# Attention in float32 on one core: q and k turned by VectorE's blocks and SBUF-to-SBUF transfers instead of TensorE, with plain float32 scores

## What is computed

```python
q = q * cos + _rotate_half(q) * sin
k = k * cos + _rotate_half(k) * sin
scores = einsum('bhqd,bhkd->bhqk', q, k) / sqrt(D)
scores = where(mask == 0, -1e9, scores)
attn = softmax(scores, axis=-1)
x = einsum('bhqk,bhkd->bhqd', attn, v) ... @ Wo
```

## Time and profile before

| | |
|---|---|
| median of 3 runs | 2615.45 us (2614.41 to 2617.41) |
| span of the profiled execution | 2614.6 us |
| TensorE busy | 2382.5 us, 91% |
| VectorE busy | 1786.3 us, 68% |
| GpSimd busy | 1512.2 us, 58% |
| ScalarE busy | 1278.9 us, 49% |
| mean granted TensorE clock | 0.967 |

### The profile page before, as it was taken

How to read it: one execution, slowest core, us unless ns; L and a number is a source line. 1 busy time by engine, 2 the same in 40 slices (tenths; PEclk the granted TensorE clock), 3 DMA queues, 4 the chain that set the end, 5 groups by cost and what they waited for, 6 DMA issues and landing times.

```text
span 2614.6 us, 41410 instructions
## 1 busy us (share of the span) xinstructions
PE 2382.5 (91%) x13005; PEld 2016.6 (77%) x13005; DVE 1786.3 (68%) x3406; ACT 1278.9 (49%) x3698; POOL 1512.2 (58%) x1567
## 2 busy tenths in 40 slices
PE   5899999998889999999887887899689999999977
PEld 4788888886778888888766776776578888888753
DVE  4677777777877777777666676563477777777752
ACT  2555555554246666666534455233245666665421
POOL 5666666665246666666535667423456666666543
PEclk9999999999999999999999999899889999999979
DMA  3234444443224233223310000259513233322344
GB/s 110 80 118 155 141 160 159 151 162 109 71 84 142 97 98 102 93 93 98 109 49 17 1 1 27 81 193 365 175 61 108 91 98 101 101 94 77 116 169 151
DMA packets 191532, 288.12 MB, mean 110 GB/s; under 512 B 15985, under 2 KB 110833, under 8 KB 188378
## 3 DMA queue, kind: packets, MB, share of 16 engines
q1 hardware_dynamic: 175584, 236.34, 27.1%
q0 software_dynamic: 10224, 42.03, 4.6%
q10 hardware_dynamic: 5514, 7.11, 0.9%
HBM read 218.80 MB, written 100.37 MB: 122 GB/s over the span
## 4 chain that ended last, share of the span: by engine, by line
PE 73%; DVE 8%; DMA 6%; POOL 5%; issue 4%; ACT 3%; SPq 0%; POOLq 0%; ACTq 0%; DVEq 0%
PE B_qkv L806 32%; PE B_out L806 19%; PE B_more L883 4%; PE B_s L863 4%; PE B_qT L852 3%; DMA slots_y<-S 3%; PE B_more L806 2%; PE B_s L864 1%; PE B_more L957 1%; DMA out_x<-rows_last 1%; PE B_s L806 1%; DVE xn L1523 1%; DVE X L1650 1%; PE B_qT L806 1%; PE B_more L855 1%
## 5 line engine op out<-in xcount | busy, mean ns | idle before, releaser
L1333 ACT ACTIVATE W<-S,nmx 128x128 f32<-128x128 f32 x768 | 298.1, 395 | 49.9 <-DVE nmx L1625 48.8
L2183 POOL TENSOR_TENSOR S<-S,mask 128x512 f32<-128x512 f32 x184 | 256.6, 1394 | 46.9 <-ACT S L1162 46.9
L1226 ACT ACTIVATE sq<-B_qkv 128x640 f32<-128x640 f32 x127 | 89.7, 706 | 380.1 <-PE B_qkv L806 380.1
L2228 POOL TENSOR_TENSOR pT_l<-W,pT_h 128x512 fp32r<-128x512 f32 x184 | 241.8, 1314 | 32.9 <-ACT pT_h L1162 30.7
L2157 POOL TENSOR_SCALAR rn<-ss 128x5 f32<-128x5 f32 x128 | 25.3, 198 | 371.3 <-DVE ss L1563 371.3
L806 PE MATMUL B_qkv<-ring_h,xnT_h 128*128 128x512 f32 x540 | 216.2, 400 | 11.3 <-DVE spare_l L1474 4.8
L2222 POOL TENSOR_TENSOR W<-W,rden 128x512 f32<-128x512 f32 x192 | 202.1, 1052 | 32.7 <-DVE rden L1630 32.6
L806 PE MATMUL B_qkv<-ring_l,xnT_h 128*128 128x512 f32 x540 | 214.5, 397 | 0.0
L806 PE MATMUL B_out<-ring_h,oT_h 128*128 128x512 f32 x516 | 206.1, 399 | 8.7 <-DVE kT L1615 4.4
L806 PE MATMUL B_qkv<-ring_h,xnT_l 128*128 128x512 f32 x540 | 212.8, 394 | 0.0
L863 PE MATMUL B_s<-kT,qT_h 128*128 128x256 f32 x768 | 191.1, 326 | 17.8 <-DVE xnT_l L1474 15.1
(11 more groups left out here) (514 smaller groups left out, 7730.5 us busy)
## 6 DMA issues: line engine op xcount, KB each, us to landing
raw<-in_pieces SPq DMA_DIRECT2D x270, 256.0 KB, 2.6
between_p<-S SPq DMA_DIRECT2D x184, 256.0 KB, 2.2
W<-between_p SPq DMA_DIRECT2D x184, 256.0 KB, 2.8
slots_x<-in_zero SPq DMA_DIRECT2D x32, 1030.0 KB, 6.0
raw<-in_experts SPq DMA_DIRECT2D x16, 768.0 KB, 6.5
w<-in_experts SPq DMA_DIRECT2D x8, 1024.0 KB, 14.0
slots_y<-S SPq DMA_DIRECT2D x31, 256.0 KB, 6.4
xn<-slots_x ACTq DMA_DIRECT2D x8, 257.5 KB, 5.8
```

The costliest lines, as they stand in the source:

```text
L1333: t = act.activation(W[:, k, cols(r)], S[:, k, cols(r)], ACT.Exp, bias=nmx[:, k, r:r + 1], accum_out=den[:, k, r:r + 1])
L2183: pool.tensor_tensor(S3, S3, m.unsqueeze(1).to_broadcast([P, R, P]), ALU.add).then_inc(*masked.now((layer, u)))
L2228: pool.tensor_tensor(heads_first(pT[1][:, :]), by_block(W[:, k, :]), heads_first(f32(pT[0][:, :])), ALU.subtract).then_inc(*p_split.now((l ...
```

## The change

For all units but the eight of `TURNED_BY_PE`:

- VectorE's stream transpose turns `qk` in blocks of 32 x 32 and writes them into `sq` (`blocks_q`, place 19 in norm layers, 22 in the rope layer). SP moves them with four SBUF-to-SBUF transfers of 80 KB, one a block row, into a new tile `qkT` (`load_q`, place 64), in which a token's four queries and its key lie side by side. The transfers wait for the scores of the unit before, since `qkT` exists once.
- ScalarE copies the keys out of `qkT` into `keys`, in the order of the blocks and scaled (`copy_k`, now in the step of the scores at place 30).
- The five transposes on TensorE, the copies and residues of q and k, and `low_scores` with its copy of scores and GpSimd's addition of the mask go. The scores are one plain float32 matmul of 128 columns a head, and VectorE adds the mask as it scales them.
- What waited for the transposes before it wrote `qk` now waits for `blocks_q` (`qk_read`); what writes `sq` waits for the landing of the four transfers (`sq_read`).
- The odd units of the steady stretch are projected into a second pair of banks, `B_turn`, and the even ones into `B_qkv` as before.

The norm weights are also laid out in the order of the blocks. The core of the diff:

```diff
@@ -152,10 +152,14 @@
                     frees=[(n, "qkv", (layer, u), i + 0.7) for n in five[0:3]] if last else ())
             if KINDS[layer] == "norm":
                 self.at(i + 1, 6 if layer == 1 and u < NB else 10, "normalise", layer, u)
-            self.at(i + 1, 50, "turn_q", layer, u)
-            self.at(i + 1, 50, "split_k", layer, u)
+            if (layer, u) in TURNED_BY_PE:
+                self.at(i + 1, 50, "turn_q", layer, u)
+                self.at(i + 1, 50, "copy_k", layer, u)
+            else:
+                self.at(i + 1, 19 if KINDS[layer] == "norm" else 22, "blocks_q", layer, u)
+                self.at(i + 1, 64, "load_q", layer, u)
+                self.at(i + 2, 30, "copy_k", layer, u)
             self.at(i + 2, 40, "scores", layer, u)
-            self.at(i + 2, 41, "low_scores", layer, u)
             self.at(i + 2, 56, "mask", layer, u)
             self.at(i + 2, 71, "exp", layer, u)
             self.at(i + 3, 9, "probs", layer, u)
...
+        with ExitStack() as besides_small_heads:
+            qkT = besides_small_heads.enter_context(nc.sbuf_tensor("qkT", [P, P, R + 1], F32))
+            keys = besides_small_heads.enter_context(nc.sbuf_tensor("keys", [P, P], F32))
...
 
         B_qkv = pb("B_qkv", 1024)
-        B_qT = pb("B_qT", 512)[:, :]
-        B_s = pb("B_s", 1024)
-        B_sc, B_kT = B_s[:, 0:512], B_s[:, 512:1024]
+        B_turn = pb("B_turn", 1024)
+        B_qT, B_kT = B_turn[:, 0:512], B_turn[:, 512:1024]
+        B_sc = pb("B_sc", 512)[:, :]
         B_more = pb("B_more", 1024)
         B_pt, B_oT = B_more[:, 0:512], B_more[:, 512:1024]
 
         def unit_bank(layer, u):
 
-            return (B_more, ("pt", "oT")) if (layer, u) in ASIDE else (B_qkv, ("qkv",))
+            if (layer, u) in ASIDE:
+                return B_more, ("pt", "oT")
+            if NB <= u < G * NB - NB and u % 2:
+                return B_turn, ("qT", "kT")
+            return B_qkv, ("qkv",)
...
+        def qk_read(layer, u):
+
+            return (qk_turned if (layer, u) in TURNED_BY_PE else q_blocks).of((layer, u))
+
+        def sq_read(layer, u):
+
+            if (layer, u) in TURNED_BY_PE:
+                return (summed if KINDS[layer] == "norm" else roped).of((layer, u))
+            return q_loaded[unit(layer, u)[3]].of((layer, u))
...
-        score_parts = B_s[:, :].rearrange("p (r a k) -> p r a k", r=R, a=2)
+        def query(r):
+
+            return qkT[:, :, r]
+
+        keys_in = qkT[:, :, R].rearrange("p (a j) -> p j a", j=BLOCKS)
+        keys_by_block = keys[:, :].rearrange("p (j a) -> p j a", j=BLOCKS)
+        sq_blocks = sq[:, :].rearrange("p (j q h) -> p h j q", j=BLOCKS, q=BLOCK)
...
             def turn_q(layer, u):
                 kind, g, b, k, vs = unit(layer, u)
                 pe.wait_ge(*{"rope": roped, "norm": normed}[kind].of((layer, u)))
-                bank_free("qT")
+                bank_free("qT", "kT")
                 for h in range(R):
                     pe.transpose(B_qT[:, cols(h)], qk[:, cols(h)], ident[:, :])
-                bank, name = key_bank(layer, u)
-                bank_free(name)
-                pe.transpose(bank, qk[:, cols(R)], ident[:, :]).then_inc(*qk_turned.now((layer, u)))
-                read["qT"], read[name] = qT_lo.of((layer, u)), kT_lo.of((layer, u))
+                pe.transpose(B_kT[:, 0:P], qk[:, cols(R)], ident[:, :]).then_inc(*qk_turned.now((layer, u)))
+                read["qT"], read["kT"] = q_copied.of((layer, u)), keys_made.of((layer, u))
 
             def scores(layer, u):
-                pe.wait_ge(*qT_lo.of((layer, u)))
-                pe.wait_ge(*kT_lo.of((layer, u)))
-                bank_free("sc", "kT")
+                if (layer, u) in TURNED_BY_PE:
+                    pe.wait_ge(*q_copied.of((layer, u)))
+                else:
+                    pe.wait_ge(*q_loaded[unit(layer, u)[3]].of((layer, u)))
+                pe.wait_ge(*keys_made.of((layer, u)))
+                bank_free("sc")
                 for r in range(R):
-                    pe.matmul(B_s[:, cols(r, 2 * P)], qT[0][:, cols(r)], kT_both[:, :], start=True, stop=False)
-                    t = pe.matmul(B_s[:, cols(2 * r)], qT[1][:, cols(r)], kT[0], start=False, stop=True)
+                    t = pe.matmul(B_sc[:, cols(r)], query(r), keys[:, :], start=True, stop=True)
                 t.then_inc(*scored.now((layer, u)))
-                read["sc"] = read["kT"] = sc_read.of((layer, u))
+                read["sc"] = sc_read.of((layer, u))
...
                     act.activation(sq[:, :], unit_bank(layer, u)[0][:, 0:HG + P], ACT.Square).then_inc(*squared.now((layer, u)))
-                    sq_reader[:] = [summed.of((layer, u))]
-                if kind == "rope":
-                    sq_reader[:] = [roped.of((layer, u))]
+                sq_reader[:] = [sq_read(layer, u)]
...
                 act.wait_ge(*qk_turned.of((layer, u)))
                 for sem, value in qT_reader:
                     act.wait_ge(sem, value)
-                copy(qT[0][:, :], B_qT).then_inc(*qT_hi.now((layer, u)))
-
-            def split_k(layer, u):
+                copy(qkT[:, :, 0:R].rearrange("p t r -> p r t"), per_head(B_qT)).then_inc(*q_copied.now((layer, u)))
+
+            def copy_k(layer, u):
                 kind = KINDS[layer]
-                act.wait_ge(*qk_turned.of((layer, u)))
+                by_pe = (layer, u) in TURNED_BY_PE
                 for sem, value in qT_reader:
                     act.wait_ge(sem, value)
-                if layer == 3 and u == 0:
-                    act.wait_ge(*kbd_made2.of(NB - 1))
-                scale = wqk[:, layer // 2:layer // 2 + 1] if kind == "norm" else 1.0
+                which = layer - 1 + (not by_pe)
+                scale = wqk[:, which:which + 1] if kind == "norm" else 1.0
                 if kind == "norm" and u == 0:
                     act.wait_ge(*const.of("wqk"))
-                copy(key_rows(layer, u, kT[0]), key_columns(layer, u), scale).then_inc(*kT_hi.now((layer, u)))
+                if by_pe:
+                    act.wait_ge(*qk_turned.of((layer, u)))
+                    copy(keys_by_block, B_kT[:, 0:P].rearrange("p (a j) -> p j a", j=BLOCKS), scale).then_inc(*keys_made.now((layer, u)))
+                else:
+                    act.wait_ge(*q_loaded[unit(layer, u)[3]].of((layer, u)))
+                    copy(keys_by_block, keys_in, scale).then_inc(*keys_made.now((layer, u)))
...
-            def low_scores(layer, u):
-
-                k = unit(layer, u)[3]
-                act.wait_ge(*scored.of((layer, u)))
-                if layer == 0 and u == 0:
-                    act.wait_ge(*const.of("mask0"))
-                if layer == 3 and u < 2:
-                    for t in range(TILES2 - 2, TILES2):
-                        act.wait_ge(*y_stored[t % 2].of((2, t)))
-                elif k in S_reader:
-                    act.wait_ge(*S_reader[k])
-                copy(per_head(S[:, k, :]), score_parts[:, :, 1, :], SCALE).then_inc(*low_scored.now((layer, u)))
...
@@ -1571,11 +1575,12 @@
                     if u < NB:
                         dve.wait_ge(*rope_in[b].of(0))
                     if u:
+                        dve.wait_ge(*sq_read(layer, u - 1))
                         dve.wait_ge(*roped.of((layer, u - 1)))
                     dve.tensor_tensor(sq3.rearrange("p h (a d) -> p h a d", a=2), bank.rearrange("p h (a d) -> p h a d", a=2),
                                       cos, ALU.mult)
                     if u:
-                        dve.wait_ge(*qk_turned.of((layer, u - 1)))
+                        dve.wait_ge(*qk_read(layer, u - 1))
...
-            def turn_q(layer, u):
-                dve.wait_ge(*qT_hi.of((layer, u)))
-                sub(qT[1][:, :], B_qT, f32(qT[0][:, :])).then_inc(*qT_lo.now((layer, u)))
-
-            def split_k(layer, u):
+            def blocks_q(layer, u):
+
+                kind = KINDS[layer]
+                dve.wait_ge(*{"rope": roped, "norm": normed}[kind].of((layer, u)))
+                if kind == "norm":
+                    dve.wait_ge(*summed.of((layer, u)))
+                dve.transpose(sq_blocks, qk[:, :].rearrange("p (h j q) -> p h j q", j=BLOCKS, q=BLOCK)
+                              ).then_inc(*q_blocks.now((layer, u)))
+
+            def mask(layer, u):
                 kind, g, b, k, vs = unit(layer, u)
-                bank = key_columns(layer, u)
-                hi, lo = (key_rows(layer, u, m) for m in kT)
-                dve.wait_ge(*kT_hi.of((layer, u)))
-                if kind == "rope":
-                    sub(lo, bank, f32(hi)).then_inc(*kT_lo.now((layer, u)))
-                else:
-                    dve.scalar_tensor_tensor(out=lo, in0=bank, scalar=wqk[:, layer // 2:layer // 2 + 1], in1=f32(hi),
-                                             op0=ALU.mult, op1=ALU.subtract).then_inc(*kT_lo.now((layer, u)))
-
-            def mask(layer, u):
-                k = unit(layer, u)[3]
```

(36 more changed lines are left out.)

63 lines of the change are left out of this document (25 added, 38 removed).

## The result

The changed kernel takes 3546.02 us (median of 4 runs, 3543.71 to 3553.4) against 2616.43 for the kernel before on the same chip: a ratio of 1.3546 with a 95% interval of 1.352 to 1.3573. It is slower by the mechanism that was foretold, and by more: 3293 was the forecast, and 3546 lies 6 us above the upper end of the range. The profiled execution has a span of 3541.5, 926.9 more than before.

What follows compares the result with a forecast made beforehand. The prediction took TensorE's work as the bound before, a ring of transfer waits after. Adding 4.25 us in 124 norm steps (527) and 2.7 in 56 rope steps (151), 678 together, to 2614.6 gave 3293 us, range 3100 to 3540.

Steps and rivals of the forecast that it cites:

- The bound before: Before the change, TensorE's own work sets the time in 184 of 192 units, at 9.06 us a step.
- The ring: Square through store, its landing, `load_p` and `load_q`'s landing to the next Square: 13.3 us norm, 11.75 rope; chance 0.84.
- the wait that the prediction put first: `copy_k` queued behind the output copy on ScalarE stalls TensorE before the scores 1.2 us a step; alone 2732 us, chance 0.07.
- The four issues: SP's issues of the four `load_q` transfers, priced at 0.33 us each after `load_p`'s issue of 0.38.
- The landing: Time for an 80 KB query transfer to land, taken as 2.0 us, with 1.5 and 2.8 as ends.
- Rope's landing: In the rope layer's sum, the landing of the query transfers, taken as 2.0 us as in the norm layers.
- Square to store: In a norm step, from ScalarE's Square to the store's issue: 6.8 us, plus 0.8 for `blocks_q`.
- The 20-byte stride: TensorE's scores read queries 20 bytes apart in `qkT`; cost bounded by nothing and a doubled scores block, 0.9 us.
- the ring's slack: In a norm step, 9.6 of 13.3 us needed, leaving 3.7 us to hide the keys' wait, stride and lower clock.
- The prediction's rival with TensorE as the bound: TensorE's work still sets the time, 0.52 us less in 184 units: 2519 us, faster; chance 0.05.
- TensorE's work: TensorE's own work a step falls to 8.54 us once the five transposes go.
- The clock: TensorE, some 64% busy, may get a lower clock; at 1.2 GHz a norm step would be 14.7 us, an upper end.

Runs made afterwards that it cites:

- Opening it at the queue: Changed kernel with SP issuing the four query transfers ahead of the load of the probabilities (place 61 for 64): 3255.0 us.
- opening it at the tile: Changed kernel with VectorE's blocks of units 10 to 55 written to a tile of their own instead of `sq`: 3133.7 us.
- both open: Changed kernel with the blocks' own tile and the query transfers issued ahead of the load of the probabilities: 3050.8 us.
- every opening that was tried: Changed kernel with own tile, query transfers first, keys' copy ahead of the output's, clears in layer 2: 2742.6 us with contiguous queries, 2817.8 us with the stride.

## Why the forecast was right in kind and short in size

- **The bound before** (TensorE, 9.05 us a step) holds: with the transfers gone and the scores at their old length the step is 9.05 again.
- **The ring, its order and its releasers** hold, leg by leg. Opening it at the queue took 2.1 us a norm step, opening it at the tile 3.2; with both open the wait that the prediction put first, the keys' copy, holds the step.
- **The four issues** are the term that failed: 2.5 us for 1.32, which is 1.2 a step and some 210 us over the 180 steps that were counted, most of the 249 by which the profiled sum was short. I priced an issue by the store's row (0.33) and the load's (0.38) and gave it no bounds, although no row showed an issue between two SBUF tiles. The landing, which the trace did not show either, had bounds and fell within them (2.3 between 1.5 and 2.8). Leaving three issues out gave 1.5 us back. What makes such an issue longer than the store's stays open: runs of 128 bytes instead of 640 changed it by 0.04 us only. The Trainium skill's estimate of 2.2 us for the landing, which the prediction set beside its sum, agrees with the 2.3, though the section that it names fits transfers issued by GpSimd and these were issued by SP.
- **Rope's landing** was taken as the norm layers'. The clears on the same queue, visible before the change, cost 0.7 us a step (50 us in the run that moved them).
- **`blocks_q`** was priced by the bytes of the other block transpose. It writes 4-byte elements 20 bytes apart, and from start to start takes 1.18 us where 0.8 stood in the sum. Square to store, 6.8 + 0.8, came out at 7.86 (7.03 in the 35 of 96 steps without a weight piece on VectorE before the store, 8.33 in the 61 that have one): the 0.3 more is within this term's error of 0.4.
- **The 20-byte stride** was bounded by a doubled scores block, and that is nearly what happened (0.77 of the 0.9), at a granted clock of 1.00. That it hides in the ring's slack was right: contiguous queries gained nothing there. In two thirds of the units there was little to hide, as at 0.50 the scores take 1.77 us with the stride and 1.70 without. The prediction's rival with TensorE as the bound would have ended well above 2519 by it. The Trainium skill (SBUF — State Buffer, Door 1: The DMA port swizzle) says that an access which leaves a 16-byte line with every element pays for it. The runs agree with 0.77 us a step at a clock of 1.00; at 0.50 the price was 0.07.
- **The copy of the keys**, 1.2 us: TensorE's idle time is 1.18, but the step is 1.5 longer by it (10.80 against 9.27). **TensorE's work** without the turns, 8.54: the shortest steps are 8.51.
- **The clock** was 0.85 in the steady windows, as the upper end had allowed for, and TensorE 76% busy, where 64% were expected and "under 70%" was to be a sign; at a lower clock most of the same work lasts longer. The ring holds none of TensorE's work, so this cost nothing: the step shortens one for one with what leaves the ring.

## What to carry to other kernels

The transfers lost by 4.7% even with every opening that was tried; what won, by 1.3%, was TensorE's turns with plain scores on contiguous queries. Before a transfer is put in the place of TensorE's work, follow its source tile to the next writer and its issue through the queue: a wait that stands ahead of it there (here the store's landing, 2 us) becomes the transfer's too. Give each issue a bound of its own: four small transfers cost 2.5 us on a queue before the last one flies. And when a layout is chosen for the transfer, ask who reads it: where TensorE turned the queries, contiguous ones kept the plain product at no cost, while the stride alone took 0.77 us a step.

## What the runs showed of the hardware

- An issue of a transfer of 80 KB between two SBUF tiles takes SP 0.60 us (median) in runs of 640 bytes and 0.64 in runs of 128 bytes; four take 2.5 and 2.7 us, and with 1 MB in flight on the same queue 2.6 and 4.45.
- Such a transfer lands 2.3 us (median) after its issue, 2.8 in runs of 128 bytes. With 1 MB in flight ahead of it on the queue, what waits for it starts 3.34 us after the end of the last issue and not 1.73.
- A plain float32 weight load of 128 columns takes 191 ns with contiguous elements and 311 with elements 20 bytes apart at a granted clock of 1.00. At 0.50 it takes 329 and 315: the strided load hardly changed with the clock.
- VectorE's block transpose of 640 columns takes 0.83 us with runs of 32 elements in its output and 1.35 with elements 20 bytes apart.
